# A two-layer decoder on one core: the order of work inside a step of the second cross attention

## The reference, cut to what matters

```python
q = (x @ w_q + b_q).reshape(B, Lq, 16, 16)
k = (context @ w_k + b_k).reshape(B, -1, 16, 16)
v = (context @ w_v + b_v).reshape(B, -1, 16, 16)
scores = einsum('bqhd,bkhd->bhqk', q, k) / sqrt(16)
weights = softmax(scores, axis=-1)
out = einsum('bhqk,bkhd->bqhd', weights, v).reshape(B, Lq, D)
return out @ w_o + b_o
```

## Time and profile before

| | us |
|---|---|
| time, median of 3 runs | 3457.3 (3453.26 to 3458.07) |
| span of the profiled execution | 3459.0 |
| second cross attention, step loop (first scores to last values) | 2627.9 to 3251 |
| PE busy over the whole span | 3138.3 (91%) |
| DVE busy | 2354.6 (68%) |
| ACT busy | 1708.5 (49%) |

### The profile page before, as it was taken

One profiled execution on the slowest core, in us unless ns is written; L12 is line 12 of the kernel. 1 busy time (PEld: TensorE's weight loads), 2 busy tenths in 40 slices (PEclk: granted clock), 3 DMA queues, 4 the chain that ended last, 5 costly groups with the idle time before them and its releaser, 6 DMA issues. The chain is left out here.

```text
span 3459.0 us, 62575 instructions
## 1 busy us (share of the span) xinstructions
PE 3138.3 (91%) x24201; PEld 1810.0 (52%) x24201; DVE 2354.6 (68%) x4987; ACT 1708.5 (49%) x2102; POOL 1731.8 (50%) x1163
## 2 busy tenths in 40 slices
PE   7999999989999999999999953958989999999797
PEld 3666666644555555555555523846654434444346
DVE  5999999945655665566656556156429978888518
ACT  3888888823434444444444441222234656666641
POOL 5999999814777777777777831322460000000012
PEclk9999999989999999999999976988997999999898
DMA  2000000020000000000000054730021111120101
GB/s 70 6 2 2 2 2 2 26 55 1 4 1 4 1 4 4 1 4 1 4 1 1 1 160 136 239 86 1 1 43 18 18 18 18 18 26 10 33 1 37
DMA packets 65530, 91.51 MB, mean 26 GB/s; under 512 B 9586, under 2 KB 55539, under 8 KB 64371
## 3 DMA queue, kind: packets, MB, share of 16 engines
q1 hardware_dynamic: 61682, 83.17, 9.5%
q0 software_dynamic: 3072, 4.34, 0.7%
q10 hardware_dynamic: 512, 0.26, 0.0%
HBM read 62.34 MB, written 10.65 MB: 21 GB/s over the span
## 5 line engine op out<-in xcount | busy, mean ns | idle before, releaser
L969 DVE TENSOR_REDUCE x0hm<-x0pM 128x1 f32<-128x400 f32 (+1 forms) x1024 | 520.8, 563 | 378.3 <-PE x0pM L871 378.2
L434 POOL TENSOR_SCALAR rows<-rows,mb 128x1024 bf16<-128x1024 bf16 x512 | 567.5, 1119 | 98.1 <-DVE mb L382 98.1
L376 DVE TENSOR_SCALAR_CACHE_REDUCE rows<-pS 128x1024 bf16<-128x1024 f32 x512 | 605.8, 1209 | 2.0 <-PE pS L312 1.5
L445 ACT ACTIVATE prT<-pP 128x1024 bf16<-128x1024 bf16 x512 | 521.9, 1024 | 110.1 <-PE pP L323 92.6
L1433 DVE TENSOR_REDUCE x1hm<-x1pM 128x1 f32<-128x400 f32 (+1 forms) x1024 | 519.1, 567 | 67.4 <-PE x1pM L1319 64.2
L1552 ACT ACTIVATE x1pr<-x1pST 128x1024 f32<-128x1024 f32 (+1 forms) x416 | 403.8, 1022 | 216.1 <-PE x1pST L1371 216.0
L831 POOL TENSOR_TENSOR x0acc<-x0acc,x0pr 128x1024 f32<-128x1024 f32 (+1 forms) x176 | 422.1, 2398 | 110.2 <-ACT x0pr L1080 95.0
L831 POOL TENSOR_TENSOR x0acc<-x0acc,o_nat 128x1024 f32<-128x1024 f32 (+1 forms) x176 | 419.1, 2381 | 72.3 <-ACT o_nat L1080 53.5
L1080 ACT ACTIVATE x0pr<-x0pST 128x1024 f32<-128x1024 f32 (+1 forms) x208 | 212.9, 1024 | 279.6 <-PE x0pST L915 279.6
L1080 ACT ACTIVATE o_nat<-x0pST 128x1024 f32<-128x1024 f32 (+1 forms) x208 | 213.0, 1024 | 278.4 <-PE x0pST L915 278.0
L2666 POOL MEMSET f_tri<- 128x128 f32 x1 | 0.2, 209 | 675.7 <-POOLq L1224 675.7
(11 more groups left out here) (367 smaller groups left out, 5125.2 us busy)
## 6 DMA issues: line engine op xcount, KB each, us to landing
m_w<-in_moe_w1T SPq DMA_DIRECT2D x16, 1024.0 KB
m_w<-in_moe_w2T SPq DMA_DIRECT2D x16, 1024.0 KB, 9.1
acc_d<-m_zero SPq DMA_DIRECT2D x8, 514.0 KB, 9.5
m_acc<-acc_d SPq DMA_DIRECT2D x8, 514.0 KB, 5.6
x1sq<-x1qh SPq DMA_DIRECT2D x32, 128.0 KB, 4.0
x1sk<-x1kh SPq DMA_DIRECT2D x32, 100.1 KB, 3.6
rows_d<-m_xr SPq DMA_DIRECT2D x1, 2176.0 KB, 9.0
g_xN<-in_x SPq DMA_DIRECT2D x1, 2048.0 KB
```

The lines of the kernel that those rows point to most:

```text
L376: nc.vector.tensor_scalar(rows[u][:, half * 1024:(half + 1) * 1024], pS[half][:, :], 1.0, None, ALU.mult, ALU.max, accum_out=mx[u][:, half ...
L434: nc.gpsimd.tensor_scalar(r, r, -1.0, mb[u][:, 0:1], ALU.mult, ALU.add).then_inc(s_df, 1)
L445: nc.scalar.activation(prT[u][:, half * 8:(half + 1) * 8, :], pP[half][:, :, :], ACT.Exp, scale=-1.0 / HD ** 0.5).then_inc(s_ex, 1)
L969: emptied(nc.vector.tensor_reduce(hm[g % 2][:, a, t, i % 8 // 2:i % 8 // 2 + 1], bank(name)[:, 0:w], AX.X, ALU.max, negate=True), name)
```

## The change

Within a step PE gets the order: scores 0, two pieces, the full-array unit, values part 0, scores 1, the other two or three pieces (with the `shift`), values part 1. The numbering of the units, and with it the banks and DVE's order, follows: the full-array unit moves ahead of the third piece. ACT's queue is written as before: exponentials 0, exponentials 1, the units of the step.

```diff
-        return parts[:2], parts[2:4], whole, parts[4:]
+        return parts[:2], whole, parts[2:]
...
-                        front, middle, whole, rest = units_in(u, kt)
+                        front, whole, back = units_in(u, kt)
                         scores(u, kt, 0)
-                        for name in front:
+                        for name in front + whole:
                             unit(name)
-                        scores(u, kt, 1)
                         if u or kt:
                             values(u * STEPS + kt - 1, 0)
-                        for name in middle:
+                        scores(u, kt, 1)
+                        for name in back:
                             unit(name)
                         if u or kt:
                             values(u * STEPS + kt - 1, 1)
-                        for name in whole + rest:
-                            unit(name)
```

## The result

| | before | after |
|---|---|---|
| time, median (lowest to highest), us | 3457.7 (3453.3 to 3459.8) | 3498.8 (3494.8 to 3503.0) |
| ratio, 95% interval | | 1.0120 (1.0106 to 1.0134) |
| span of the profiled execution, us | 3459.0 | 3499.6 |
| step loop, first scores to last values, us | 622.9 | 666.5 |
| halved clock within the loop, after its start in half 0, us | 6.8 | 47.8 |

The change makes the kernel 41 us slower; 3491 was forecast, 3469 to 3511 the range. The profiled executions differ by 40.6 us, the loops by 43.6. The 3 us between them lie outside the loop, before its first scores and after its last values.

The account below looks back on a forecast made before the run. Neither PE nor DVE alone but a ring of waits through both was taken as the bound. Terms -1 + 12.9 + 6.4 + 7 + 4.6 + 6 gave +35.9, taken as 34: 3457.3 + 34 = 3491 us, range 3469 to 3511.

Parts of the forecast that it names:

- (a): Plain steps, some 110 of 208: the wait only changes its place, -1 us; bounds -26 and +10.
- (b): Eight q and k projections: high part queued behind exponentials 1, step 7.34 us, +12.9 us in all; bounds 0 and +20.
- (c): Four `turn` units, halves 9 to 12: steps of 5.06 us, +6.4; `norm` and `out` unchanged, -4 to +3.
- (d): Ends of 14 halves: `shift` +0.3 us, later output copy +0.2 to +0.4; together +7, between 0 and +14.
- (e): Last 15 steps without pieces: values wait for exponentials, plain steps 2.19 us; +4.6 us, between +2 and +8.
- (f): Clock falling to half after longer PE gaps: three more falls, +6 us, between 0 and 12 more (+24).
- a ring: Plain step: PE and DVE wait for each other through a piece's bank, 2.76 us; PE alone 2.53, DVE alone 2.41.
- rival 2: Whole loop: the clock falls with every long gap, 12 falls, +24 instead of +6 us, 3509; chance 0.14.
- Rival 1: Plain steps: third back piece doesn't wait for its bank, 2.53 us a step, -26 us, total 3462 or 3455; chance 0.08.
- Rival 3: Projection and `turn` steps: stalls mostly hidden by slack in DVE's queue, about +18 us, 3475; chance 0.12.

Follow-up runs that it names:

- the first experiment: Changed kernel with ACT's queue taking the q and k high parts and `turn` copies between exponentials 0 and exponentials 1: 3463.0 us, ratio 1.0019 to the kernel before.

## Why the prediction was right, and where its sizes were off

The forecast's mechanism held at each place; I go by its terms, with the loop's +43.6 us.

| term | forecast | measured | from |
|---|---|---|---|
| (a) plain steps | -1 | 0 | 2.77 to 2.78 us a step in both |
| (b) eight projections | +12.9 | about +12 | the three steps with the next at the full clock: 10.10 - 8.52 = 1.58, then 1.46 and, without the `shift`, 1.4 |
| (c) four `turn` | +6.4 | +6.5 | 5.08 + 2.78 against 3.37 + 2.87, times 4 |
| (c) eight `out` | 0 | -1.5 | a pair 0.27 or 0.11 us shorter |
| (c) `norm`, 14 halves | 0 | -2.7 | steps 3 and 4 0.19 us shorter |
| (d) `shift` and output copy, 14 halves | +7 | +11.5 | steps 11 and 12 +0.22, steps 0 to 2 +0.61 |
| (e) last steps | +4.6 | +5.0 | 34.95 - 28.1 without 2.2 us of low clock, and 0.36 in half 14 |
| (f) clock | +6 | +12 to 14 | the rest of the loop; and step by step, below |

(a) The step kept its length, the wait changed its place. That the wait is a ring, and not PE at its end, rests on two runs that open it, one in the changed kernel from DVE's side and one in the kernel before from PE's, at 2.54 and 2.55 us.

(b), (c) The chain from scores 0 was to bring the back piece at 6.40 us and the next step at 7.34; the trace has 6.39 and 7.34 for the first q projection, and the other three steps of half 4 are 7.21, 7.19 and 6.97 us. For the `turn` it was 5.06, measured 5.08. That halves 4 and 5 together would grow by 12 us was short: they grew by 18.6, with the clock and the ends of the halves in it.

(d) was argued from two causes; the trace shows a part of each. Step 11 with the `shift` takes 3.86 us (3.24 before), of which step 12 gives 0.40 back: +0.22 where +0.3 was forecast. Step 1, in which the first values of the half wait for the output copy, takes 2.95 (2.40), and step 2 0.09 more: +0.6 where +0.2 to +0.4 was forecast. There PE first waits for exponentials 1 of step 0, whose scores the new order issues later, and then for the copy, which ACT starts only behind them (step 1 of half 6, changed kernel):

```profile
2895.97 0.19 PEld L1386 LDWEIGHTS x1pO<-x1pr,x1v 128*32 128x32 f32 x8 [0.65 <-ACT x1pr L1550]
2896.00 0.64 PE L1386 MATMUL x1pO<-x1pr,x1v 128*32 128x256 f32 x8 [0.33 <-ACT x1oc L1557]
```

The wait for the copy is listed for the loop; it was not in the table of before, where 0.34 us fourteen times is new:

```profile
PE x1pO L1386 <- ACT x1oc L1557: 4.7, 14, 0.4
```

No experiment took either cause away alone, so the shares rest on the lengths of the steps. `norm` and `out` together gave 4.2 us, a little beyond the lower bound of -4 in (c). That (d) came 4.5 us above its forecast and these 4.2 below theirs, so that the two cancel in the sum, is luck.

(e) Plain steps came at 2.19 us, as worked out. Before, plain ones were 1.66 us and not ACT's 1.84, so that the reading of ACT as the pace was wrong there; the sum suffered little, because other steps before were longer. The two `out` behind a `turn` take 3.79 us (2.72 to 2.77 before), +1.0 where +0.9 was forecast. In the run with ACT's queue changed these two are 3.05, so 1.5 of the 5 us belong to (c)'s mechanism.

(f) is the mis-sized term: three more falls were taken, there were six more. The price of a fall was right in kind, 2 us, but several lasted longer than one stretch. Added up by steps: half 9 is 4.2 us longer than the same half in the run with the last 15 steps changed, halves 10 and 12 1.1 and 1.2, and the first steps of half 15 2.2 us longer than with ACT's queue changed. For half 5 no run has this order at the full clock; the 45.1 us of the run with ACT's queue changed and 1.9 us for each of four projections make 52.7 against 61.1, so I estimate about 8 us. Together that is some 17 us; less 2.6 for the one fall of before (7.97 + 3.25 against 5.05 + 3.61) some 14, against the 13 that the table leaves. None of the seven lay in half 4, where the forecast looked for some: three were in half 5, one each in halves 9, 10 and 12, and the last one at the start of the last half. That one followed no stall of ACT's queue but a wait for the DMA that brings the last maxima:

```profile
3254.34 0.19 PEld L1371 LDWEIGHTS x1pST<-x1sq,x1sk 64*128 64x128 f32 x2 [1.77 <-DMA x1sq<-x1nt]
```

The run with ACT's queue changed has this wait too, 1.76 us, and no fall; the one with the unit at the end of the step has it and a fall of 6.8 us. So some 2 of the 16 or 17 us that the first experiment gave back by the clock aren't due to the repair. By the number of falls the result lies between the forecast (four) and rival 2 (twelve), seven; by the time too: 3498.8 between 3491 and 3509.

The rule of the Trainium skill's page "TensorE: Matmul & The Clock Gate", section "HAM oscillation — how this bites in real kernels", by which such gaps are too short to bring the clock down, would have left out these 12 to 14 us; seven falls after gaps of at most 2.8 us speak against taking it as a bound. Rival 1, the opening ring, needed the front reductions to end 0.3 us earlier. The run with narrow reductions shows that this point exists; the changed kernel, with its plain steps at 2.78 us, doesn't reach it. Rival 3, hidden stalls, is ruled out by the terms (b) and (c).

Three places of the working don't hold. The 2 us taken off the sum of 35.9, because (d) and (f) might overlap, went the wrong way: the terms came in full, at +41.1 in time. The upper bound of (a), +10, doesn't follow from its words; a tenth of 2.77 us in 55 steps would be 15. And the chances of the rivals give 0.02 for faster, where 0.03 is stated.

## What to carry to other kernels

When a unit is moved in one engine's order, walk through the queue of every engine that empties its buffer: if this work stands there behind an instruction whose input the new order issues later, it stalls all that share the buffers. Where two engines seem both near their ends, write the ring of waits with its terms and look for what lies in it without need: here two matmuls ahead of a piece that waits, and moving them one place was worth 1%. Idle time of TensorE is paid twice when the clock falls after it, so a stall that is repaired can give back more than its length (40 us for 23 here, of which some 2 are a fall that the repair doesn't explain).

## What the runs showed of the hardware

The clock fell from 2.4 to 1.2 GHz after single waits of 1.8 us, and in another execution of the same instructions it did not: the stretches of 3.4 us shown held 1.98 us of busy PE in the one and 1.97 in the other. It stayed at 2.4 GHz through a stretch with 1.02 us. No run here says what decides. A fall of 10.2 us cost 4.2 us, one of 3.4 us 1.1 to 1.2 us, less than half of the stretch; I take it that some of the slowdown lies under waits, which no run isolates. The ring through DVE had these terms: a reduction of 400 columns lasts 0.57 us, but the next one starts 0.48 us after it, and a weight load follows 0.05 us after the reduction that it waits for.
